# Filling TensorE's planned gaps in an attention and routing block with identity products

## The chip, the cores and the metric

One Trainium2 chip, one of its cores. The engines are PE (TensorE), DVE (VectorE), ACT (ScalarE), POOL (GpSimd) and SP (SyncE, which here only issues transfers). The metric is the device time of one launch in microseconds, as a median of runs.

## The reference

Four sequences of 1024 tokens and 256 features go through two layers. Each layer is attention and then a feed-forward part:

- layer 0: causal attention with 16 heads of 16 features, rotary embedding and a window of 64 keys; residual and layer norm; a gated feed-forward part that mixes each token with the one before it, `r * (relu(k)**2 @ W_v)`; residual and layer norm
- layer 1: linear attention over random features, `out = q_feat @ (k_feat.T @ v)`; residual and layer norm; then a block with its own layer norm, full causal attention (softmax over up to 1024 keys), another layer norm, and a mixture of 8 experts where each token goes to its two best, with 1024 places for each expert, counted in token order; a last layer norm

The order of the tokens fixes the place of each token at its expert, so the four sequences pass the router one after another.

## The kernel before, in words

The kernel has three stages: a short set-up (loads and a few transposes), the attention block that does everything up to the router for all four sequences (`attend_and_pass_on`), and the experts with the last norm. The change is in the attention block.

The block's work is cut into steps. A step is named by its kind and its place, as `("max", g, t, x)`. The 16 heads of a sequence are four groups of four; windowed and full attention of all sequences give 32 groups `g`, and each group has two halves `h` of 512 queries. The PE steps that matter here:

- `proj` (L849) projects one row tile of 128 tokens; `turn` (L868) transposes
- `max` (L876, L879, L883): scores for the row maximum. An identity times a mask first writes the mask into the bank, then the scores are added. DVE's `reduce` (L1277) reads the bank; POOL's `parts` (L1322 to L1325) splits the maximum into three bf16 parts, PE's `rows` (L889) transposes them, ACT's `lines` (L1050) copies them out, SP's `spread` sends them into `b_qk`
- `exp` (L896): the scores again, less the maximum; ACT's `power` (L1026) takes the exponential; POOL's `clear` (L1372) masks; `values` (L910) multiplies by the values; `collect`, `out` (L918) and `divide` (L1299, L1301) turn and normalise
- the layer steps: `r` (L659) and `k0` (L670) are products of the feed-forward part, `x1_turn`, `o_turn`, `oc_turn`, `h_turn` and `z_turn` (L665) are transposes of 4 times 128 x 128 in fp32, `oc_pj` (L659) is the output projection, and `logits` (L763) and `position` (L769 to L772) belong to the router. DVE's `mix_k` is L1155, the router's `place` on DVE ends at L1249

No engine decides anything at run time. A planner, `Planner.arrange`, walks a model of the block on the host: every step has a cost in us written by hand, an engine, and the steps that it comes after. It gives each engine a fixed order (`plan.program`). At each moment an idle engine takes, among the steps that are ready, the one with the longest chain behind it (`urgent`).

PSUM has eight banks of 512 fp32 columns. A PE step that fills a bank takes the one that the model frees first (`plan.bank`); `plan.after` keeps the step that had the bank before, and `left_by` names the step of DVE, ACT or POOL whose end gives the bank back. In the model a step is ready when both its inputs and a bank are there:

```python
if self.takes(x):
    b = min(bank_free, key=lambda k: bank_free[k])
    ready = max(ready, bank_free[b])
```

On PE a step of the program becomes this sequence: first `plan.wait_bank(pe, x, s)`, a wait until the bank has been read by its last reader; then the step's own waits on its inputs; then its matmuls, of which the last one increments a semaphore. PE works through its program in order.

Of the kernel before, what the change touches and what calls it, by code (L numbers as in the profile page):

```python
# [32 lines left out]
P = 128  # L33
# [19 lines left out]
CT = CAP // P  # L53
NEG = -2.0 ** 100
EPS = 1e-5
EARLY = 1
BANK = 512
DROPPED = 65536.0
# [36 lines left out]
class Planner:  # L95
# [20 lines left out]
    def add(self, x, engine, cost, *after):  # L116
        mine = self.kinds.setdefault(x[0], [])
        self.steps[x] = Step(engine, cost, [y for y in after if y is not None] + mine[-1:])
        mine.append(x)

    def arrange(self):

        steps = self.steps
        order = {x: n for k in self.kinds.values() for n, x in enumerate(k)}
        followers = {x: [] for x in steps}
        for x, st in steps.items():
            for y in st.after:
                followers[y].append(x)
        waiting = {x: len(followers[x]) for x in steps}
        urgent, ends = {}, [x for x in steps if not followers[x]]  # L130
        while ends:
            x = ends.pop()
            st = steps[x]
            urgent[x] = st.cost + max([urgent[y] + (0.0 if steps[y].engine == st.engine else self.LANDING[x[0]]
                                                    if st.engine == "SP" else self.LATE[st.engine])
                                       for y in followers[x]], default=self.AHEAD.get((x[0], x[-1]), 0.0))
            for y in st.after:
                waiting[y] -= 1
                if not waiting[y]:
                    ends.append(y)  # L140

        queues = {}
        for kind, xs in self.kinds.items():
            queues.setdefault(steps[xs[0]].engine, []).append([list(reversed(xs))])
        free_at, done, banks, bank_free = {}, {}, {}, {b: 0.0 for b in self.BANKS}
        self.program = {e: [] for e in ("PE", "DVE", "ACT", "POOL", "SP")}
        self.bank, self.after, used = {}, {}, {}
        issue_of = {self.left_by(x): x for k in self.TAKEN_BY for x in self.kinds.get(k, []) if self.takes(x)}
        now, left = 0.0, len(steps)
        while left:  # L150
            soonest, moved = None, False
            for engine, lists in queues.items():
                at = free_at.get(engine, 0.0)
                best = None
                for (q,) in lists:
                    if not q:
                        continue
                    x = q[-1]
                    if any(y not in done for y in steps[x].after):
                        continue  # L160
                    ready = max([done[y] + (0.0 if steps[y].engine == engine else self.LANDING[y[0]] if steps[y].engine == "SP"
                                            else self.LATE[steps[y].engine]) for y in steps[x].after], default=0.0)
# [3 lines that stand above are left out]
                    start = max(at, ready)  # L166
                    if start > now:
                        soonest = start if soonest is None else min(soonest, start)
                    elif best is None or urgent[x] > urgent[best[0]]:
                        best = (x, q)  # L170
                if best is not None:
                    x, q = best
                    q.pop()
                    left -= 1
                    moved = True
                    end = now + steps[x].cost
                    free_at[engine] = done[x] = end
                    self.program[engine].append(x)
                    if self.takes(x):
                        b = min(bank_free, key=lambda k: bank_free[k])  # L180
                        self.bank[x], self.after[x] = b, used.get(b)
                        used[b] = x
                        bank_free[b] = float("inf")
                    if x in issue_of:
                        bank_free[self.bank[issue_of[x]]] = end + self.LATE[engine]
            if not moved:
                assert soonest is not None
                now = soonest
        self.order = order
        self.length = max(done.values())  # L190
# [18 lines left out]
class Plan(Planner):  # L209
# [45 lines left out]
    def xa_left(self, b):  # L255


        return ("out1", 3, b - 1) if b == EARLY else self.last_projected(b, True)

# [53 lines left out]
    def describe(self):  # L313
# [14 lines left out]
        for b in range(1, B):  # L328
            add(("source", b), "SP", 6.0, ("h_turn", 1, NC - 1, b - 1))
            for y in range(2):  # L330
                for c in range(NC):
                    add(("fetch", y, c, b), "PE", 0.435, *[] if b == EARLY else [("source", b), ("out1", 3, b - 1)])
                    add(("refill", y, c, b), "ACT", 0.52, ("fetch", y, c, b))
# [57 lines left out]
        def softmax(g, h):  # L391
            mine = (g, h)
            cells = self.query_cells(g, h)
            for t, a, e in cells:
# [11 lines left out]
                if t == self.batches[b][-1][0]:  # L406
# [5 lines left out]
                *([] if self.place_of(g) else [self.known("x4_out", self.batch[g] - 2)] if windowed[g] else  # L412
                  [("o_turn", 1, EARLY), ("back", self.group_of(EARLY, True, 0), 1)] if not self.batch[g] else
                  [self.known(*x, self.batch[g] - 1) for x in (("z_out",), ("z_turn", 1, 1), ("x4", 3))]))
# [66 lines left out]
    def describe_layer(self, b):  # L481
        def add(x, engine, cost, *after, other=()):


            self.add(x + (b,), engine, cost, *[y + (b,) if y and y[0] in LAYER_KINDS else y for y in after], *other)
# [5 lines left out]
        for k in range(4):  # L491
            add(("pj", k), "PE", 1.73, ("o_take", k // 2), ("keep", near[0], k // 2))
            add(("y1", k), "DVE", 1.4, ("pj", k), other=[("source", b)] if b == EARLY else [])
        self.describe_norm(b, "n1", "y1", ("x1",))
# [58 lines left out]
        for h in range(2):  # L553
            for c in range(NC):
                before = self.last_projected(b - 1, False) if b else self.last_projected(EARLY, True)
                add(("h_turn", h, c), "PE", 0.435, ("h_act", 4 * h + 1), ("h_dve", 4 * h + 3), before)
# [32 lines left out]
def attend_and_pass_on(nc, u, s, x_dram, later, early_in, slots_gathered, slots_dram, z_dram, x4_dram):  # L589


    plan = Plan(ORDER)
# [4 lines left out]
    def o_of(g):  # L597
        return u.o if windowed[g] and plan.batch[g] != EARLY else u.y

# [43 lines left out]
    def bank_of(*x):  # L643
        return u.psum[:, plan.bank[x], :]
# [7 lines left out]
    def four(h):  # L652
        return slice(4 * h, 4 * h + 4)
# [33 lines left out]
    with nc.Block() as block:  # L687
        @block.sync
        def _(sp):
            for x in plan.program["SP"]:  # L690
                kind = x[0]
                b = x[-1]
                if kind == "source":
                    done(sp, b - 1, "h_turn", 1, NC - 1)
                    sp.dma_start(u.src[:, :, :], x_dram[b:b + 1, :, :].rearrange("o (t p) d -> p (o t) d", p=P)).then_inc(s.src_in, 16)
                elif kind == "load":
                    _, g, a, slot, y = x
                    part = [slot in slots for slots in SLOTS_OF[a]].index(True)
                    sp.wait_ge((s.high_done, s.mid_done, s.low_done)[part], 4 * (g // 2) + (4 if y is None else 2 * y + 2))
# [41 lines left out]
        def _(pe):  # L741
            for x in plan.program["PE"]:
                kind = x[0]
                if x in plan.bank:
                    plan.wait_bank(pe, x, s)
                if kind in LAYER_KINDS:
                    out = bank_of(*x)
                    x, b = x[:-1], x[-1]
# [10 lines left out]
                    elif kind == "logits":  # L759
                        done(pe, b, "z_take", 1, 1)  # L760
                        for t in range(NT):
                            for c in range(NC):
                                ins = pe.matmul(out[:, E_ * t:E_ * t + E_], u.xtr[:, c, P * t:P * t + P], u.wgate[:, c, :],  # L763
                                                start=(c == 0), stop=(c == NC - 1))
# [43 lines left out]
                    elif kind == "kv":  # L808
                        done(pe, b, "k_feat", 3)
                        done(pe, b, "v1_sum", 3)  # L810
                        for c in range(NC):
                            for t in range(NT):
                                ins = pe.matmul(out[:, P * c:P * c + P], u.kfeat[:, D * t + P * c:D * t + P * c + P],
                                                u.o[:, t, P * c:P * c + P],
                                                start=(t == 0), stop=(t == NT - 1))
# [19 lines left out]
                n = order[x]  # L835
# [34 lines left out]
                elif kind == "max":  # L870
# [4 lines left out]
                    if windowed[g]:  # L875
                        pe.matmul(out, u.id16[:, :], u.mask_q[:, :, WQ - (e - a):WQ], start=True, stop=True,  # L876
                                  skip_group_check=True)
                    elif last:
                        pe.matmul(out[:, :, P * t - a:P * t - a + P], u.id16[:, :],  # L879
                                  u.causal_q[:, :].unsqueeze(1).broadcast_to([P, len(heads), P]), start=True, stop=True,  # L880
                                  skip_group_check=True)
                    for i, h in enumerate(heads):
                        ins = pe.matmul(out[:, i, :], q[0:KS, h, P * t:P * t + P], q[0:KS, HG + h, a:e],  # L883
                                        start=not last, stop=True, skip_group_check=True)
# [6 lines left out]
                elif kind == "exp":  # L891
# [3 lines left out]
                    for i, h in enumerate(heads):  # L895
                        ins = pe.matmul(out[:, i, :], q[0:KM, HG + h, P * t:P * t + P], q[0:KM, h, a:e],  # L896
                                        start=True, stop=True, skip_group_check=True)
# [178 lines left out]
        def _(dve):  # L1076
# [11 lines left out]
            for x in plan.program["DVE"]:  # L1088
                kind = x[0]
                if kind in LAYER_KINDS:  # L1090
# [16 lines left out]
                    elif kind.endswith("_var"):  # L1107
# [6 lines left out]
                        if name == "n3":  # L1114
                            dve.tensor_scalar(w.var[:, 1, four(h)], w.mv[:, four(h), 1], 1.0 + EPS, EPS * EPS, ALU.mult, ALU.add)
                        ins = dve.tensor_scalar(w.var[:, 0, four(h)], w.mv[:, four(h), 1], EPS, None, ALU.add)
                    elif kind.endswith("_scale"):
# [554 lines left out]
def last_norm(nc, u, s, x4_dram, out_dram):  # L1672
# [4 lines left out]
    with nc.Block() as block:  # L1677
# [36 lines left out]
        def _(dve):  # L1714
            link = dve_chain(dve, s.chain)

            def statistics(h):
# [5 lines left out]
                for i in range(4 * h, 4 * h + 4):  # L1723
                    ins = dve.bn_aggr(u.last_mv[:, i, :], u.last_bn[:, i, :])  # L1724
                link(ins)
                dve.tensor_scalar(u.last_var[:, 4 * h:4 * h + 4], u.last_mv[:, 4 * h:4 * h + 4, 1], EPS, None, ALU.add  # L1726
                                  ).then_inc(s.var_ready, 1)
# [259 lines left out]
```

## Time and profile before

| | |
|---|---|
| median of 3 runs | 1914.5 us (1913.64 to 1915.02) |
| the profiled execution | 1915.56 us, span 1913.8 us |
| PE busy | 1713.6 us (90% of the span) |
| DVE, ACT, POOL busy | 1018.5, 879.8, 831.4 us |
| granted TensorE clock, mean over the span | 0.948 |

The span is the time from the first to the last instruction. The granted clock is a share of TensorE's full 2.4 GHz: 1.00 is 2.4 GHz, 0.50 is 1.2 GHz. "Idle before" in a row of the timeline is the time for which the engine had nothing to do before this instruction, and behind the arrow stands what ended it. Ends of matmuls are modelled, with the latency of each one in them, so consecutive matmuls overlap; the rate of a run of n equal matmuls is (length of the run less the length of one) over n - 1.

### The profile page before, as it was taken

The page shows a single profiled execution, that of the slowest core. Times are in us where ns is not written, and L with a number is a line of the kernel's source. Part 1 is how long each engine was busy: PE and PEld are TensorE (multiplying, and loading weights), DVE is VectorE, ACT ScalarE, POOL GpSimd, SP SyncE. Part 2 cuts the span into 40 slices and gives each one's busy share as a digit, 9 for nine tenths or more (in the row PEclk, how much of TensorE's full clock was granted, in tenths as well). Part 3 has the DMA queues.
Part 4 walks back from the last instruction along what each step waited for, and adds up shares of the span by engine and source line. Part 5 has one row for each costly group of instructions (what it writes and reads, how often), then busy time and mean ns, then how long its engine had stood idle before and what let it go on. Part 6 is the DMA issues. An engine that isn't in the chain of part 4 may idle for free. (4 is left out here: it accounts for less than half of the span.)

```text
span 1913.8 us, 32830 instructions
## 1 busy us (share of the span) xinstructions
PE 1713.6 (90%) x10804; PEld 1106.0 (58%) x10804; DVE 1018.5 (53%) x2375; ACT 879.8 (46%) x1855; POOL 831.4 (43%) x1247
## 2 busy tenths in 40 slices
PE   4798998999999999999989999998279999999970
PEld 3565765665477666556756545545246776666750
DVE  3457676868566986847698677775101110001115
ACT  2355463657755364765536566765031222222202
POOL 4574564522377552248663243324434333234220
PEclk9899999999999899999999999999589999999995
DMA  5615235032344222254502223420313332333115
GB/s 190 92 19 67 35 79 68 14 55 68 53 74 100 24 34 35 68 68 69 112 2 40 52 50 41 68 67 22 121 59 85 83 69 49 70 85 88 23 17 181
DMA packets 93059, 124.17 MB, mean 65 GB/s; under 512 B 14065, under 2 KB 63153, under 8 KB 92737
## 3 DMA queue, kind: packets, MB, share of 16 engines
q1 hardware_dynamic: 78560, 105.24, 26.8%
q0 software_dynamic: 14336, 16.83, 5.3%
q8 instruction: 94, 1.54, 0.4%
q14 instruction: 69, 0.56, 0.1%
HBM read 45.70 MB, written 25.56 MB: 37 GB/s over the span
## 5 line engine op out<-in xcount | busy, mean ns | idle before, releaser
L1026 ACT ACTIVATE b_probs<-b_psum 128x512 f32<-128x512 f32 (+3 forms) x896 | 417.9, 544 | 179.3 <-PE b_psum L896 177.7
L1277 DVE TENSOR_REDUCE b_mneg<-b_psum 128x2 f32<-128x384 f32 (+5 forms) x608 | 333.5, 593 | 94.0 <-PE b_psum L883 92.4
L1372 POOL TENSOR_SCALAR_AFFINE_SELECT b_probs<-b_probs 128x512 f32<-128x512 f32 (+1 forms) x400 | 240.0, 611 | 314.8 <-ACT b_probs L1026 304.3
L883 PE MATMUL b_psum<-b_qk 96*128 96x192 bf16 (+4 forms) x1280 | 298.9, 300 | 6.0 <-DVE b_before L1249 2.7
L896 PE MATMUL b_psum<-b_qk 99*128 99x192 bf16 (+5 forms) x1344 | 262.8, 290 | 9.7 <-DMA b_qk<-b_mrow 6.4
L1656 DVE TENSOR_TENSOR b_ye<-b_psum,b_b2b 128x512 f32<-128x512 f32 x32 | 22.1, 692 | 428.9 <-PE b_psum L1611 428.9
L1635 ACT ACTIVATE b_hid<-b_psum,b_b 128x512 f32<-128x512 f32 x128 | 88.0, 687 | 317.9 <-PE b_psum L1602 317.9
L1564 POOL DMA_INDIRECT before_last_norm<-b_ye,b_ids x64 | 99.5, 1555 | 301.0 <-DMA before_last_norm<-b_ye,b_ids 156.2
L1611 PE MATMUL b_psum<-b_w,b_hid 128*128 128x256 f32 x1024 | 222.4, 379 | 0.8 <-ACT b_hid L1635 0.8
L1602 PE MATMUL b_psum<-b_xgt,b_w 128*128 128x512 f32 x512 | 221.7, 594 | 0.0
L1611 PEld LDWEIGHTS b_psum<-b_w,b_hid 128*128 128x128 f32 x1024 | 193.9, 190 | 27.6 <-ACT b_hid L1635 1.6
L910 PE MATMUL b_psum<-b_probs,b_v 128*32 128x192 f32 (+4 forms) x2688 | 198.1, 416 | 2.3 <-POOL b_probs L1372 2.0
L883 PEld LDWEIGHTS b_psum<-b_qk 96*128 96x128 bf16 x1280 | 125.5, 101 | 100.7 <-issue 27.5
L1388 POOL TENSOR_TENSOR b_rot<-b_product 128x128 f32<-128x128 f32 x256 | 115.4, 483 | 133.4 <-DVE b_product L1260 57.1
L1277 DVE TENSOR_REDUCE b_mhalf<-b_psum 128x1 f32<-128x512 f32 x256 | 165.1, 682 | 13.1 <-PE b_psum L883 12.7
L1602 PEld LDWEIGHTS b_psum<-b_xgt,b_w 128*128 128x128 f32 x512 | 97.6, 191 | 119.4 <-issue 119.0
L896 PEld LDWEIGHTS b_psum<-b_qk 99*128 99x128 bf16 x1344 | 113.5, 98 | 88.1 <-issue 19.8
L910 PEld LDWEIGHTS b_psum<-b_probs,b_v 128*32 128x32 f32 x2688 | 69.6, 110 | 90.1 <-issue 65.0
L1260 DVE TENSOR_TENSOR b_product<-b_psum,b_cossin 128x512 f32<-128x512 f32 x128 | 87.9, 688 | 59.9 <-PE b_psum L849 54.9
L849 PE MATMUL b_psum<-b_wqkv,b_xt 128*128 128x384 f32 x320 | 116.8, 493 | 0.6 <-ACT b_xt L938 0.4
L876 PE MATMUL b_psum<-b_mask_q,b_id 128*128 128x384 bf16 (+1 forms) x256 | 84.9, 334 | 7.7 <-DMA b_qk<-b_split 5.7
L879 PE MATMUL b_psum<-b_causal_q,b_id 128*128 128x128 bf16 (+2 forms) x352 | 88.7, 252 | 3.0 <-ACT b_probs L1026 1.1
(212 smaller groups left out, 2431.6 us busy)
## 6 DMA issues: line engine op xcount, KB each, us to landing
b_qk<-b_split SPq DMA_DIRECT2D x372, 128.0 KB, 4.9
b_w<-in_W SPq DMA_DIRECT2D x16, 1024.0 KB, 7.8
b_src<-in_x SPq DMA_DIRECT2D x4, 1024.0 KB, 6.2
before_last_norm<-b_early SPq DMA_DIRECT2D x4, 1024.0 KB, 4.9
b_o<-before_last_norm SPq DMA_DIRECT2D x4, 1024.0 KB, 5.4
before_last_norm<-b_o SPq DMA_DIRECT2D x4, 1024.0 KB, 4.5
normed<-b_y SPq DMA_DIRECT2D x4, 1024.0 KB, 5.2
b_rows<-before_last_norm SPq DMA_DIRECT2D x8, 512.0 KB, 7.8
```

What stands on the lines that cost most here:

```text
L849: ins = pe.matmul(u.psum[:, plan.bank[x], 0:384].rearrange("p (a g y) -> p a g y", a=3, g=2), x_rows[:, c, P * t:P * t + P], (u.wqkv0 if n ...
L879: pe.matmul(out[:, :, P * t - a:P * t - a + P], u.id16[:, :], u.causal_q[:, :].unsqueeze(1).broadcast_to([P, len(heads), P]), start=True, ...
L883: ins = pe.matmul(out[:, i, :], q[0:KS, h, P * t:P * t + P], q[0:KS, HG + h, a:e], start=not last, stop=True, skip_group_check=True)
L896: ins = pe.matmul(out[:, i, :], q[0:KM, HG + h, P * t:P * t + P], q[0:KM, h, a:e], start=True, stop=True, skip_group_check=True)
L910: ins = pe.matmul(sums_of(g, h2)[32 * h:32 * h + 32, a - BANK * h2:e - BANK * h2], u.v[:, g % 4, t, (HD + 1) * h:(HD + 1) * h + 32], probs ...
L1026: act.activation(probs_of((g, h2, t), a, e)[:, heads[0]:heads[-1] + 1, :], bank, ACT.Exp, scale=SCALE).then_inc(s.exp_done, 1)
L1277: dve.tensor_reduce(out, in_bank(("max",) + x[1:], heads, e - a), AX.X, ALU.max, negate=True).then_inc(s.max_read, 1)
L1372: ins = pool.affine_select(out=block, in_=block, pattern=[[0, HG], [1 if ahead else -1, z - y]], compare_op=ALU.is_ge, fill=none, base=y - ...
L1388: ins = pool.tensor_tensor(out[:, :, :, HALF * y:HALF * y + HALF], straight[:, :, :, HALF * y:HALF * y + HALF], crossed[:, :, :, HALF * (1 ...
L1564: pool.indirect_dma_start(out=x4_dram, out_offset=bass.IndirectOffsetOnAxis(ap=u.ids[:, column:column + 1], axis=0), in_=u.ye[q][:, t, :], ...
L1602: ins = pe.matmul(u.psum[:, k % 4, :], u.w1[e % 2][:, c, P * n:P * n + P], u.xgt[:, c, BANK * h:BANK * h + BANK], start=(c == 0), stop=(c ...
L1611: ins = pe.matmul(u.psum[:, q, D * t:D * t + D], u.hid[:, n, P * (2 * q + t):P * (2 * q + t + 1)], u.w2[e % 2][:, n, :], start=(n == 0), s ...
```

## The change

The planner now keeps, for every step, how long its engine stood idle in the model before it (`self.idle`). When PE comes to a step that takes a bank and whose planned idle time was above 1.0 us, it issues, behind the wait for the bank and ahead of the step's own waits, a number of 128 x 128 bf16 products of the identity with itself into the first 128 columns of that bank. The step overwrites them. Their number is 0.6 of the planned idle time over 0.064 us each.

```diff
+LEAST_IDLE = 1.0
+FILLED = 0.6
+FILLER = 0.064
...
         self.bank, self.after, used = {}, {}, {}
+        self.idle = {}
...
                 at = free_at.get(engine, 0.0)
-                best = None
+                best, at = None, free_at.get(engine, 0.0)
...
                     end = now + steps[x].cost
+                    self.idle[x] = now - at
                     free_at[engine] = done[x] = end
...
                 if x in plan.bank:
                     plan.wait_bank(pe, x, s)
+                    for n in range(int(FILLED * plan.idle[x] / FILLER) if plan.idle[x] > LEAST_IDLE else 0):
+                        pe.matmul(u.psum[:, plan.bank[x], 0:P], u.id16[:, :], u.id16[:, :], start=True, stop=True,
+                                  skip_group_check=True)
```

The order of every engine and every bank stay as they were.

## Rows read from the trace of the kernel before

**Rows 1.** The page: busy time, share of the span and instructions of each engine

```profile
PE 1713.6 (90%) x10804; PEld 1106.0 (58%) x10804; DVE 1018.5 (53%) x2375; ACT 879.8 (46%) x1855; POOL 831.4 (43%) x1247
```

**Rows 2.** Stretches: length, busy time of each engine, clock, DMA share

```profile
core 0: us, PE busy (x) PEld busy (x) DVE busy (x) ACT busy (x) POOL busy (x), PEclk, DMA share, GB/s
24.00:1335.00 1311.00, 1239.03 (x9029) 783.39 (x9028) 935.92 (x2073) 747.68 (x1648) 630.49 (x1087) 0.97 0.32 56
...
51.60:54.80 3.20, 2.88 (x14) 2.00 (x15) 1.80 (x4) 0.28 (x1) 0.00 (x0) 0.50 1.00 142
58.40:61.70 3.30, 3.03 (x8) 1.86 (x9) 0.00 (x0) 0.59 (x1) 0.13 (x1) 0.50 1.07 133
89.20:99.20 10.00, 7.88 (x47) 5.88 (x48) 3.68 (x8) 3.12 (x8) 3.75 (x7) 0.50 1.07 128
154.00:157.20 3.20, 3.20 (x9) 2.67 (x10) 2.07 (x4) 1.75 (x3) 1.37 (x2) 0.50 0.12 41
174.50:177.70 3.20, 3.20 (x5) 1.23 (x4) 2.42 (x5) 0.00 (x0) 1.98 (x2) 0.50 1.06 124
300.80:307.40 6.60, 4.96 (x16) 3.46 (x15) 0.68 (x2) 0.93 (x2) 0.41 (x1) 0.50 0.62 97
...
1335.00:1403.10 68.10, 17.38 (x112) 15.73 (x113) 10.22 (x64) 7.99 (x14) 38.32 (x39) 0.50 0.41 133
```

**Rows 3.** Timeline of PE: steps whose inputs came last

```profile
44.30 0.37 PE L876 MATMUL b_psum<-b_mask_q,b_id 128*128 128x256 bf16 x1 [5.05 <-DMA b_qk<-b_split]
...
50.87 0.38 PE L889 MATMUL b_psum<-b_id,b_mparts 128*128 128x128 bf16 x4 [2.16 <-POOL b_mparts L1325]
...
58.67 0.59 PE L889 MATMUL b_psum<-b_id,b_mparts 128*128 128x128 bf16 x4 [2.50 <-POOL b_mparts L1325]
...
173.74 0.67 PE L670 MATMUL b_psum<-b_early,b_wk 128*128 128x512 f32 x1 [3.05 <-DVE b_early L1155]
```

**Rows 4.** Timeline of PE: steps whose bank came last

```profile
335.33 0.80 PE L659 MATMUL b_psum<-b_wr,b_early 128*128 128x256 f32 x1 [2.02 <-DVE b_mhalf L1277]
...
457.13 0.44 PE L665 MATMUL b_psum<-b_id,b_src 128*128 128x128 f32 x2 [0.80 <-ACT b_mrow L1050]
...
958.65 0.39 PE L883 MATMUL b_psum<-b_qk 96*128 96x512 bf16 x1 [1.97 <-DVE b_before L1249]
...
979.07 0.48 PE L659 MATMUL b_psum<-b_wr,b_early 128*128 128x256 f32 x1 [2.86 <-DVE b_mneg L1277]
```

**Rows 5.** Source view of L889: durations in ns, smallest, median, largest

```profile
L889 PE MATMUL b_psum<-b_id,b_mparts x256: 216/219/314, 50.9 to 1298.1; 128*128 128x128 bf16 x128
```

**Rows 6.** Timeline of PE: two bf16 matmuls of 128 columns, clock 0.50

```profile
44.46 0.42 PE L883 MATMUL b_psum<-b_qk 96*128 96x128 bf16 x2
```

**Rows 7.** Stretches behind the places of rows 4

```profile
338.30:456.30 118.00, 117.55 (x701) 72.76 (x700) 92.66 (x195) 71.72 (x149) 43.70 (x61) 1.00 0.22 37
457.20:512.90 55.70, 55.59 (x410) 30.52 (x410) 39.67 (x72) 39.49 (x84) 21.54 (x45) 1.00 0.21 54
638.70:655.00 16.30, 15.16 (x63) 10.14 (x63) 15.69 (x29) 3.47 (x6) 12.65 (x13) 0.79 0.04 3
```

**Rows 8.** Timeline of PE: steps with no idle time, and one behind them

```profile
517.60 0.64 PE L910 MATMUL b_psum<-b_probs,b_v 128*32 128x512 f32 x4
...
891.39 0.91 PE L896 MATMUL b_psum<-b_qk 99*128 99x64 bf16 x10 [1.08 <-DMA b_qk<-b_mrow]
```

**Rows 9.** Timeline of PE: the router's last steps; the logits of a sequence earlier

```profile
1299.15 3.64 PE L763 MATMUL b_psum<-b_wgate,b_early 128*128 128x8 f32 x32
...
1336.67 1.94 PE L665 MATMUL b_psum<-b_id,b_y 128*128 128x128 f32 x8 [6.04 <-DVE b_y L1136]
1339.65 1.94 PE L665 MATMUL b_psum<-b_id,b_y 128*128 128x128 f32 x8 [1.04 <-ACT b_y L980]
1342.55 6.97 PE L763 MATMUL b_psum<-b_wgate,b_early 128*128 128x8 f32 x32 [0.96 <-ACT b_early L938]
...
1352.83 0.17 PE L769 MATMUL b_psum<-b_chosen,b_upto 128*128 128x8 bf16 x1 [3.32 <-DVE b_chosen L1215]
```

## The prediction

> **What bounds the kernel now.** I read the page first: PE is busy for 90% of the span, DVE for 53% [rows 1]. The stretch view narrows it to the attention block, 24 to 1335 us: PE 1239 of 1311 us, DVE 936, at a mean clock of 0.97 [rows 2]. The reader is to see two losses of TensorE there: about 72 us of idle time, and 0.03 x 2 x 1311 = 79 us spent at half clock. Walking the stretch view along the block, these 79 us are 15 stretches of 3.4 to 10.2 us; six of them are shown [rows 2]. The router's last steps and the wait for the experts run at half clock altogether (1335 to 1403). Last I read the timeline of PE around each idle time, to see what ended it [rows 3, 4].
>
> A stretch at half clock of which PE is busy for b us costs at most b/2, if PE sets the time there.
>
> **What is added.** The number of fillers follows from the planner's own arithmetic, worked through with the costs in the listing: 27 steps have a planned idle time above 1.0 us and a bank. They get 493 products. No order, bank or wait changes.
>
> *Price of one.* Four bf16 matmuls of 128 columns with 128 x 128 weights take 0.38 us at full clock (at 50.87) [rows 3], one of them 0.216 [rows 5]: (0.38 - 0.216)/3 = 0.055 us each, weight load hidden. At half clock two take 0.42 us [rows 6], one 0.314 (the largest in rows 5): 0.107 us each. So 493 are 27 us of TensorE at full clock. Whether they cost anything depends on where the idle time lies relative to `wait_bank`, since they stand behind it.
>
> *(a) The step waits for its inputs (15 steps, 319 fillers).* The bank was free long before, and what ended the idle time was a transfer, POOL or DVE with an input [rows 3]. The fillers start when PE gets there: 57 before the first `max` (3.1 of 5.05 us), 30 and 32 before the first two `rows` (1.65 of 2.16, 1.76 of 2.50), 22 before `k0` (1.2 of 3.05). They fit, by 0.6 of the plan: cost 0. What hides them is the idle time itself; with it gone, they would cost 17.5 us.
>
> *(b) The step waits for its bank (8 steps, 113 fillers).* In the planner these eight start exactly when the bank comes free; in the trace the idle time before them ends with the instruction that reads the bank: `r` waits for a reduce of the maxima (L1277), `h_turn` for `lines` (L1050), `max` of group 24 for the router's `place` (L1249) [rows 4]. Here the fillers come after the idle time. The input is there, the real matmuls stand queued behind them, and behind these everything on PE. Price 113 x 0.055 = 6.2 us. Part counts in full: 22 before `r` of sequence 1, 10 and 10 before two `h_turn`, 14 before `r` of sequence 3. Behind the first two PE is busy for 117.55 of 118.0 and 55.59 of 55.7 us [rows 7], and it is as full behind the other two, so nothing takes the delay back: 56 x 0.055 = 3.1 us. The other four (11, 10, 13 and 23) lie where DVE is the fuller engine, 15.69 of 16.3 us against 15.16 for PE [rows 7]; PE waits for DVE again soon. Of their 57 x 0.055 = 3.1 us I count a third, 1.0; the bounds are 0 and 3.1.
>
> *(c) The plan has idle time, the trace has none (4 steps, 61 fillers).* PE runs later than planned, so bank and input are both there, as at the `values` at 517.60 [rows 8]. 17 fillers before a `values` at 888 are taken back by the 1.08 us that PE then waits for a transfer issued earlier (891.39) [rows 8], and 23 before a `values` at 84.6 by an idle time of POOL's making. The 11 at 517.60 count, 0.6, and half of 10 at 619, 0.3. Sum 0.9 us; bounds 0 and 3.4.
>
> Cost of (b) and (c): 3.1 + 1.0 + 0.9 = **5.0 us**, bounds 3.1 and 9.6.
>
> **What the clock gives back.** Only fillers of (a) stand in idle time, so only they can hold the clock. Of each half-clock stretch behind such a place:
>
> - 51.6 to 54.8, after 2.16 us of idle [rows 2, 3]: the 30 fillers leave 0.5 us. I take the clock as held. But DVE reads each pair of scores more slowly than a warm PE makes them, and the first transfer had only just landed, so of 2.88/2 = 1.4 us I count 0.4.
> - 58.4 to 61.7, after 2.50 us: held, 3.03/2 = 1.5, PE is then busy without a break; 1.3.
> - 89.2 to 99.2: DMA share 1.07, PE waits for transfers; 0.2 of 3.9.
> - 154 to 157.2, only 11 fillers ahead: one chance in three of 1.6; 0.55.
> - 174.5 to 177.7, after 3.05 us with 22 fillers: 0.4 of 1.6; 0.6.
> - 300.8 to 307.4: 9 fillers, at the edge of it, of 2.5; 0.4.
>
> The first fall, at 41.3 us, gives nothing: behind it PE waits for transfers. The eight other stretches follow places of (b), or places without fillers. Sum: 3.45 us, bounds 0 and (2.88 + 3.03 + 7.88 + 3.20 + 3.20 + 4.96)/2 = 12.6.
>
> *The router's end.* Everything from `z_turn` to `place` of the last sequence is one chain, and it runs at half clock: its logits take 6.97 us where those of the sequence before took 3.64 [rows 9]. The 30 fillers in the 6.05 us before it end 4 us too early to hold the clock. But 15 and 12 fillers between the two `z_turn` and the logits make PE busy without a break for 6 us. TensorE came back to full clock after such runs elsewhere (58.4 to 61.7, PE busy 3.03 of 3.3). I expect full clock for somewhat over half of the logits: 2.0 of 3.3 us. Against it, at half clock 15 x 0.107 = 1.6 us fill a gap of 1.04, less the 0.2 by which transposes overlap: 0.35 late, 0.1 more before the logits, and 35 x 0.107 = 3.75 in the 3.32 before `position`, 0.2. Net gain **1.4 us**, bounds -0.7 (no return of the clock) and 3.3.
>
> **The sum.** 5.0 - 3.45 - 1.4 = +0.15 us. Against the profiled execution of 1915.56 us that is 1915.7; this execution lies 1.06 above the median of the runs, so 1914.65, **1914.7 us** as a median.
>
> **A rule against the change.** After idle times of 2.16 and 2.50 us TensorE fell to half clock [rows 2, 3]. The Trainium skill, page "TensorE: Matmul & The Clock Gate", section "Why this matters for your kernels", asks only that there be no idle gaps over about 3 us between bursts. By this trace shorter ones matter too; by the page, the fillers in 23 of the 27 places would protect nothing. As a mechanism of this kernel: only the four idle times above 3 us (44.30, 173.74, 1336.67, 1352.83) [rows 3, 9] bring a gain, 0.6 + 1.4, and the rest only cost: 5.0 - 2.0 = +3.0, 1917.5 us.
>
> **The rivals.**
>
> - *Faster: the clock is worth its full price.* Every one of the six stretches is held and PE sets the time in all of them: 5.0 - 12.6 - 1.4 = -9.0, 1905.5 us. For it: PE is 78 to 100% busy in five of the six. Against it: the DMA share of 1.07 in two of the largest, the few fillers before 154 and 300.8. It decides from gains of 8.8 us up.
> - *Slower: the fillers do not hold the clock*, so the change doesn't do what it is built for. Gains 0, the router's end 0.7 late: 5.0 + 0.7 = +5.7, 1920.2 us. For it: they cover only 0.6 of the planned gap, and the largest delays of (b) sit where PE is full. Against it: bf16 products with the mask ran from 44.30 us at half clock [rows 3, 6], and by 50.87 four products took the 0.38 us of full clock: such products bring the clock back. If DVE hides nothing either, 9.6 + 0.7, 1924.8 us. It decides when less than 1.2 of the 4.85 us comes.
> - *The rule above*: 1917.5 us.
> - *The router's end only loses*: 5.0 - 3.45 + 0.7, 1916.8 us.
>
> **How the numbers follow.** A measurement of this kernel can tell from no change about 0.2%, 3.8 us. The forecast has 0.50, the faster rival 0.15, no hold of the clock 0.20 (0.04 of it at the far value), the rule 0.08, the router's end 0.07. Faster: 0.15 and 0.02 from the forecast's edge, 0.17. Slower: 0.20 and 0.02, 0.22. Within: 0.61. The range leaves out most of the faster rival and the far value: 1908.5 to 1921.0. The forecast's own is 1911 to 1918.
>
> **What would show it.** The trace of after should have: fillers at 0.055 us each, 22 of them directly behind the idle time before `r` of sequence 1, which stays 2 us, and `r` 1.2 us later than the work before it; no idle time in front of fillers in the first `rows`; full clock after about 51 and 58 us, half clock still after about 335, 618, 936 and 960; the last logits in about 5 us. The prediction is wrong if the stretches of (b) disappear too, if DVE's places take back no delay, or if PE-full stretches turn out to have slack.

## The result, and the profile after

The changed kernel took 1904.39 us (median of 6 runs, 1900.55 to 1911.71) beside 1914.76 us for the kernel before (6 runs, 1913.3 to 1916.6): ratio 0.9947, 95% interval 0.9927 to 0.9966. That is 10.4 us faster, and below 1908.5, the low end of the range. It was measured twice more, in the experiments below, and came out less: 0.9977 (0.9963 to 0.9990) and 0.9965 (0.9952 to 0.9978). All 30 runs of it have a mean of 1907.1 us (standard error 0.7), all 98 runs of the kernel before 1913.3 (0.3): **6.2 us, 0.32%, faster**. The first figure was a good draw of the one against a poor draw of the other. That the changed kernel is faster, by more than the 0.2% that the prediction called the least that can be told, holds in the mean of all runs.

The profiled execution of after is the slowest of its six, 1911.71 us, span 1910.0. It is read here for places, not for the total. The page, as [rows 1]:

```profile
PE 1731.8 (91%) x11297; PEld 1130.5 (59%) x11297; DVE 1017.4 (53%) x2375; ACT 879.0 (46%) x1855; POOL 828.5 (43%) x1247
```

PE has 11297 - 10804 = 493 more matmuls, as counted from the planner. The stretch view of after, as [rows 2]; the columns are those shown there:

```profile
24.00:1334.00 1310.00, 1254.72 (x9459) 804.43 (x9459) 935.07 (x2073) 746.99 (x1649) 627.89 (x1087) 0.98 0.32 56
54.10:57.30 3.20, 3.20 (x20) 2.46 (x19) 3.04 (x7) 0.00 (x0) 0.00 (x0) 0.50 1.08 123
91.60:98.20 6.60, 6.17 (x34) 4.93 (x35) 3.09 (x6) 2.73 (x7) 3.76 (x6) 0.50 1.07 129
146.20:149.40 3.20, 2.77 (x24) 2.16 (x24) 1.63 (x4) 2.16 (x4) 1.74 (x3) 0.50 0.00 0
171.20:177.20 6.00, 5.97 (x20) 3.77 (x21) 4.67 (x13) 1.59 (x3) 3.89 (x4) 1.00 1.07 126
296.40:303.00 6.60, 5.87 (x25) 4.68 (x24) 0.68 (x2) 1.13 (x2) 0.62 (x1) 0.50 0.59 94
1334.00:1402.00 68.00, 23.12 (x180) 20.59 (x181) 9.94 (x64) 9.72 (x15) 39.96 (x41) 0.55 0.42 137
```

The mean clock of the block rose to 0.98. The half-clock stretches at 58, 154 and 174 us are gone, the one at 89 is shorter, that at 51 stands at 54, that at 300 is still there, and one stands at 146 where there was none.

The timeline of PE; the fillers are L752. First places where the input came last, as [rows 3]:

```profile
44.96 0.28 PE L884 MATMUL b_psum<-b_mask_q,b_id 128*128 128x256 bf16 x1 [2.49 <-DMA b_qk<-b_split]
...
47.41 1.84 PE L752 MATMUL b_psum<-b_id 128*128 128x128 bf16 x30
50.28 0.40 PE L897 MATMUL b_psum<-b_id,b_mparts 128*128 128x128 bf16 x4 [1.03 <-POOL b_mparts L1333]
...
56.57 2.34 PE L752 MATMUL b_psum<-b_id 128*128 128x128 bf16 x32
58.79 0.40 PE L897 MATMUL b_psum<-b_id,b_mparts 128*128 128x128 bf16 x4
...
168.12 1.39 PE L752 MATMUL b_psum<-b_id 128*128 128x128 bf16 x22
171.23 0.70 PE L675 MATMUL b_psum<-b_early,b_wk 128*128 128x512 f32 x1 [1.72 <-DVE b_early L1163]
```

Thirty take 1.84 us: (1.84 - 0.22)/29 = 0.056 us each. They lie at the front of the idle time, and the rest of it (1.03, 1.72) stays. Before the second `rows` (58.79) none stays: there the first part of the 32 ran at half clock, and they took 2.34 us. In `e9_again`, at full clock, they took 1.95 and left 1.14. Then places where the bank came last, as [rows 4]:

```profile
331.10 2.53 PE L752 MATMUL b_psum<-b_id 128*128 128x128 bf16 x22 [2.02 <-DVE b_mhalf L1285]
333.42 0.65 PE L664 MATMUL b_psum<-b_wr,b_early 128*128 128x256 f32 x1
...
453.94 0.73 PE L752 MATMUL b_psum<-b_id 128*128 128x128 bf16 x10 [0.80 <-ACT b_mrow L1058]
454.50 0.50 PE L670 MATMUL b_psum<-b_id,b_src 128*128 128x128 f32 x3
...
957.78 2.02 PE L752 MATMUL b_psum<-b_id 128*128 128x128 bf16 x23 [1.98 <-DVE b_before L1257]
959.59 0.64 PE L891 MATMUL b_psum<-b_qk 96*128 96x512 bf16 x1
```

Here the same idle time as before, 2.02, 0.80 and 1.98 us, stands ahead of the first filler, and the real matmul follows the last filler directly. The router's end, as [rows 9]:

```profile
1335.40 1.94 PE L670 MATMUL b_psum<-b_id,b_y 128*128 128x128 f32 x8 [4.39 <-DVE b_y L1144]
1337.13 1.81 PE L752 MATMUL b_psum<-b_id 128*128 128x128 bf16 x15
1338.73 1.91 PE L670 MATMUL b_psum<-b_id,b_y 128*128 128x128 f32 x8
1340.44 1.00 PE L752 MATMUL b_psum<-b_id 128*128 128x128 bf16 x12
1341.52 4.58 PE L771 MATMUL b_psum<-b_wgate,b_early 128*128 128x8 f32 x32
1345.95 3.89 PE L752 MATMUL b_psum<-b_id 128*128 128x128 bf16 x35
```

The logits take 4.58 us where they took 6.97. The 35 fillers after them ran at half clock, 3.89 us, and leave no idle time before `position`.

### The profile page after: what moved, and what is told of

The parts are those of the page before. It is cut to its first block and busy times, and to the rows that moved or that the text cites. A ratio compares the mean times of both kernels' runs of the same rounds, so it can differ in the third digit from the quotient of the medians.

```text
span 1910.0 us, 33797 instructions
## 1 busy us (share of the span) xinstructions
PE 1731.8 (91%) x11297; PEld 1130.5 (59%) x11297; DVE 1017.4 (53%) x2375; ACT 879.0 (46%) x1855; POOL 828.5 (43%) x1247
```

## The experiments

Twelve kernels ran, ten of them with other fillers and two unchanged copies of the changed kernel. Each has a ratio against runs of the kernel before on the same chip. "Half-clock time" is 2 x (1 - granted clock) x span, as a mean over all timed runs of a kernel; it is 193.5 us for the kernel before (92 runs) and 153.8 us for the changed one (30 runs). It includes what lies behind the block: in the profile of before 68 us from 1335 on, the router's last steps and the wait for the experts, and 53 us from 1861 to the end, where PE is idle.

**Input or bank.** The planner also keeps how long the bank was free before the step started; `e1_inputs` takes one sign of it, `e2_bank` the other.

```diff
+                        self.bank_early[x] = now - bank_free[b]
...
-... if plan.idle[x] > LEAST_IDLE else 0):
+... if plan.idle[x] > LEAST_IDLE and plan.bank_early[x] > 0.01 else 0):     # e2_bank: <= 0.01
```

> Only the 19 steps whose bank is free before their inputs in the plan get their fillers (380); the 8 whose bank comes last get none. Theory A, the 113 fillers behind a bank wait are a delay of 3 to 5 us and the rest gives all of the gain: ratio to before about 0.992 (-13 to -15 us). Theory B, the fillers at those 8 steps also keep the clock, or their delay is taken back by waits for DVE: about 0.9945 or worse (-10 us or less).

> Only the 8 steps whose bank comes last get their 113 fillers. Theory A: +3 to +5 us (ratio 1.0015 to 1.0025), and the clock falls where it fell before. Theory B: between -3 and +1 us, with fewer falls of the clock.

Measured: `e1_inputs` 1901.53 us, 0.9936 (0.9914 to 0.9957); half-clock time 156 us. `e2_bank` 1917.02 us, 1.0025 (1.0012 to 1.0038), 4.8 us slower; half-clock time 192 us, as before. `e1_inputs` alone does not decide: it lies between the numbers of the two theories, and its interval holds both. `e2_bank` decides for theory A, as it lies in A's +3 to +5 us and outside B's: behind a bank wait the fillers are delay, and over whole runs they hold no clock. A row of `e2_bank`, timeline of PE:

```profile
334.75 2.53 PE L753 MATMUL b_psum<-b_id 128*128 128x128 bf16 x22 [2.03 <-DVE b_mhalf L1286]
337.07 1.14 PE L665 MATMUL b_psum<-b_wr,b_early 128*128 128x256 f32 x2
```

**By region.** A counter `pe_step` over PE's program limits the places: `pe_step < 100` for `e3_start`, `pe_step > 2500` for `e4_end`, and between them with an early bank for `e5_middle`.

```diff
-            for x in plan.program["PE"]:
+            for pe_step, x in enumerate(plan.program["PE"]):
...
+... and pe_step < 100 else 0):
```

> Only the five places before 90 us get fillers (160). The prediction's sum gave 1.9 us for them. If a kept clock is worth its full price at the start, the stretches at 51.6, 58.4 and 89.2 give up to 6.9 us: ratio 0.9965. If transfers and DVE set the time there, -1 to -2 us, 0.9993.

> Only the router's last four steps get fillers (92). The prediction's sum: -1.4 us, logits in about 5 us. If the clock is back for all of the logits, -2.5 to -3 us; if it never comes back, +0.7 us.

> Only the ten places between 100 and 1330 us whose bank is early get fillers (128). The prediction's sum: 1.55 us of clock against 0.9 of delay, -0.7 us. What the runs with all early banks, the start alone and the end alone leave for them (12.2 less 2.7 less 1.7): about -8 us, ratio 0.996.

Measured: start 0.9986 (0.9971 to 1.0001), -2.7 us, half-clock time 176 us; end 0.9991 (0.9974 to 1.0007), -1.7 us, 186 us; middle 0.9970 (0.9956 to 0.9984), -5.7 us, 182 us. The first two are not clear of nothing by themselves. The middle is, and lies far above the 0.7 us of the prediction, if below the 8 us that the other runs left for it.

**Only real gaps, and more of them.** `e6_real_gaps` drops the four places of (c) as well. `e7_more` has `FILLED = 0.9`; `e8_more_places` adds `LEAST_IDLE = 0.4` to that, and asks for a bank that is early by more than 0.2 us (not shown): 30 places, 620 fillers.

```diff
+... and plan.bank_early[x] > 0.01 and pe_step not in (84, 854, 1068, 1589) else 0):
...
-FILLED = 0.6
+FILLED = 0.9     # e7_more and e8_more_places
```

> As e1_inputs, without the four places of (c) where the trace has no idle time (15 places, 319 fillers). If those 61 fillers are a delay of 0.9 to 3.4 us: -13 to -15 us against before, ratio 0.9925. If they also keep the clock: -12 or less.

> The 15 places with 0.9 of the planned idle time in place of 0.6 (about 480 fillers). If the clock is what pays: fewer half-clock us than e6_real_gaps, and 1 to 3 us faster than it. If the fillers now outrun the gaps: as fast or slower than it.

> As e7_more, and also places with a planned idle time of 0.4 to 1.0 us whose bank is early (some 15 more). If the clock pays: the fewest half-clock us of all, -15 to -18 us, ratio 0.991. If short gaps have no bearing on the clock: as e7_more.

Measured: `e6_real_gaps` 1903.81 us, 0.9955 (0.9939 to 0.9972), half-clock time 156; `e7_more` 1907.93 us, 0.9975 (0.9964 to 0.9985), 157; `e8_more_places` 1906.08 us, 0.9953 (0.9934 to 0.9971), 146. None of the three came as far as its expectation with the clock paying (-13 to -15, 1 to 3 us below `e6_real_gaps`, -15 to -18). In `e7_more`, half as many fillers again held no more clock and lost time; its profile shows them outrunning gaps (48 before the second `rows`, with no idle time left). The additional places of `e8_more_places` did lower the half-clock time, by 10 us, and its mean time is 3.6 us below that of `e7_more` (standard error 1.6) and 0.6 above that of `e6_real_gaps` (1.9). The delay is that of the 0.9; the additional places with 0.6 were not tried.

**The changed kernel again, and the logits.** `e9_again` is an unchanged copy. `e10_logits` is `e6_real_gaps` with two fillers between the row tiles of each logits step.

```diff
                         for t in range(NT):
+                            for n in range(2 if t else 0):
+                                pe.matmul(out[:, BANK - P:BANK], u.id16[:, :], u.id16[:, :], start=True, stop=True,
+                                          skip_group_check=True)
```

> The changed kernel once more, beside runs of the kernel before on the same chip. The steps whose length the profiles give (start -3.3, 126 to 230 -1.7, 430 to 500 -1.5, router's end -2.3, bank waits +3) sum to -5.8 us; the first measurement gave -10.4. If the sum is right and the first measurement fell on slow runs of the kernel before: -5 to -8 us, ratio 0.996 to 0.997. If a gain is missing from the sum: 0.995 or less.

> As e6_real_gaps, and two identity products ahead of each of the last seven row tiles of every logits step (14 a step, 56 in all), where PE is busy with products of 8 columns and the clock falls behind them at 613, 933 and 1297 us. If it is the clock that pays, and the columns that TensorE streams hold it: fewer half-clock us by 10 to 15, and 2 to 5 us faster than e6_real_gaps. If busy time alone counts: 14 x 0.055 x 4 = 3.1 us slower, half-clock time as before.

Measured: `e9_again` 1907.61 us, 0.9977 (0.9963 to 0.9990). `e10_logits` 1905.25 us, 0.9961 (0.9945 to 0.9978), half-clock time 160: no better than `e6_real_gaps` in either. In its profile the clock still fell during the logits, at 614 and 935 us. The fall at 1270 stands in another place, where PE waited 2.46 us for a transfer; and behind the logits of 1299 the kernel before had no fall in its profile either. A miss: so few products do not hold the clock there, and whether more would pay was not tried.

**The best version.** All early banks but the `values` at 84.6 us, and the changed kernel beside it.

> The 18 places whose bank is early, without the values step at 84.6 us, whose 23 fillers cost 1.28 us in the profiles. Sum of the segments: -8.8 us against before, ratio 0.9954, and 3 us faster than the changed kernel beside it. If the fillers behind bank waits cost nothing in whole runs: as the changed kernel.

> The changed kernel, unchanged, beside e11_best on the same chip. Sum of the segments: -5.8 us, ratio 0.997. The first measurement would be 0.9947.

Measured: `e11_best` 1902.22 us, 0.9931 (0.9916 to 0.9945); `e12_third` 1906.08 us, 0.9965 (0.9952 to 0.9978). The intervals do not meet: without the fillers behind bank waits the kernel is faster. (`e11_best` also lacks the 23 at 84.6; `e1_inputs` has them and is as fast.) Together the 18 runs of `e1_inputs`, `e6_real_gaps` and `e11_best` have a mean of 1902.75 us (standard error 0.8), 4.35 us below the changed kernel and 10.6 below the kernel before.

**What a fall costs.** The fourteen profiles (before, after, twelve runs) give one more experiment for nothing: the order of PE's steps is the same in all, so the time from the start of one step to the start of another can be set side by side. Where the clock does not fall it repeats closely: 344.0 to 453.6 us is 109.4 to 109.6 in all fourteen. Lengths in us, from the starts in the timelines; "without" is for four kernels that have no fillers there (always before and `e2_bank`, and two of `e3_start`, `e4_end` and `e5_middle`), "changed" for its three profiles (after, `e9_again`, `e12_third`):

| stretch of the kernel before | without | changed | counted in the prediction |
|---|---|---|---|
| 44.30 to 51.92 (first `max` until the second transfer) | 7.63, 8.15, 7.66, 7.69 | 7.71, 7.74, 7.73 | 0 |
| 51.92 to 58.67 (second `max` to its `rows`) | 6.75, 7.38, 7.38, 7.38 | 6.12, 5.74, 5.74 | 0.4 |
| 58.67 to 72.6 (`rows`, then 14 steps of the projection) | 13.92, 14.10, 15.17, 14.93 | 12.42, 12.43, 12.49 | 1.3 |
| 72.6 to 107.81 | 35.22, 34.19, 34.33, 33.66 (the last has the 9 ahead of 107.81) | 35.28, 33.31, 34.11 | 0.2 for 89 |
| 107.81 to 152.16 | 44.35, 44.36, 44.93, 44.36 | 45.49, 44.28, 44.27 | in the 0.55 for 154 |
| 152.16 to 173.74 | 21.57, 19.90, 20.53, 19.91 | 19.25, 19.90, 19.90 | the rest of it |
| 173.74 to 178.94 (two `k0`) | 5.21, 5.21, 5.15, 3.51 | 3.54, 3.54, 3.54 | 0.6 |
| 303.78 to 330.9 | 27.15, 27.51, 28.18, 28.11 | 26.99, 25.31, 25.31 | 0.4 |
| 1336.67 to 1352.83 (`z_turn` to `position`) | 16.16, 16.16, 16.16, 16.16 | 14.24, 14.49, 12.14 | 1.4 |

The two `k0` are the cleanest: 5.15 to 5.21 us at half clock, 3.51 to 3.54 at full, whatever else the kernel has (in one kernel without fillers the clock happened to be full there). And one that has no fillers in any kernel, from 1099.5 to 1117.6 us: 18.01 to 18.02 us in the four profiles where the clock fell in it, 16.55 to 16.57 in the ten others. One fall of 3.4 us costs 1.45 to 1.67 us here, nearly half of it, where PE is full.

The same profiles tell whether the fillers or luck kept the clock. Each stretch has four kernels without the fillers ahead of it and ten with them. From 58.67 to 72.6 the clock fell or was down for a time in all four, and in none of the ten. At the two `k0` it was three of four and none of ten, from 51.92 to 58.67 four of four and six of ten, from 303.78 to 330.9 four of four and four of ten. From 1336.67 to 1352.83 it was down throughout in the four, and for part of the time in the ten.

The same view prices the bank waits. From 330.9 to 344.0 us, across `r` of sequence 1, it is 13.06, 13.32, 13.33, 13.32 us without, and 14.12, 14.49, 14.50, in `e2_bank` 14.40, with the 22 fillers: 1.1 us. The clock was down for 3.4 to 3.5 us in all of these, and the fillers themselves took 2.53 us in two of them: part of the work that ran at half clock without them ran at full clock behind them. Three kernels without these fillers were no faster there (`e1_inputs`, `e10_logits`, `e11_best`: 14.65 to 14.68), as the clock was down for 6.8 us; why is not known. The stretch from 453.6 to 561.3 us is 107.5 to 107.7 without and 108.12 in `e2_bank`, with the 10 before `h_turn`: 0.5 us.

## Why the prediction was wrong

Point by point, by its own steps.

- *Price of one filler*: 0.055 us counted, 0.056 measured; at half clock (2.53 - 0.31)/21 = 0.106, counted 0.107. Right.
- *(a) They cost nothing in the idle time before an input*: right at 0.6 of the plan where they run at full clock (152.16 to 173.74, with the 22 before `k0`, is 19.90 us with and without them); wrong at 0.9.
- *(b) The bank waits*: right in place, mechanism and size. Counted 4.1 us; `e2_bank` measured 4.8, and the runs without them are 4.35 us faster than those with them. Single places: 1.1 for 1.2, 0.5 for 0.55.
- *(c) Places without idle time*: 0.9 us counted. The 23 before the `values` at 84.6 delay it by 1.28 us, and the idle time behind takes it back, as the prediction had it: from 58.67 to 107.81 us `e9_again`, with them, took 45.74 us and `e6_real_gaps`, without, 46.02. (The clock was down for 3.4 us of it in both.) The expectation of `e11_best`, that they cost 1.28 us of the whole, was wrong. `e6_real_gaps` is not faster than `e1_inputs`: the other three cost too little to be seen.
- ***What the clock gives back* is the step that failed.** The prediction: "Sum: 3.45 us, bounds 0 and (2.88 + 3.03 + 7.88 + 3.20 + 3.20 + 4.96)/2 = 12.6", and 1.4 for the router's end, 4.85 together. Measured: the changed kernel's 6.2 us and the 4.35 that its bank waits cost are 10.6 us of gain. The table has 9.9 of them, each as the mean of without less the mean of changed. By the prediction's terms: 1.4 for 0.4 counted (51.6), 2.1 for 1.3 (58.4), 0.1 for 0.2 (89.2), 0.6 for 0.55 (154), 1.2 for 0.6 (174.5), 1.9 for 0.4 (300.8), and 2.5 for 1.4 (the router's end). The rest, 0.7, is less than the standard error of the 10.6 (0.9).

The mechanism stood, so the sum was mis-sized, in four ways. The first: a discount for another engine. For 51.6 us it said "DVE reads each pair of scores more slowly than a warm PE makes them ... I count 0.4". In `e9_again` the clock is full there (timeline of PE):

```profile
52.83 0.32 PE L884 MATMUL b_psum<-b_mask_q,b_id 128*128 128x384 bf16 x1 [2.03 <-DMA b_qk<-b_split]
...
55.32 0.33 PE L891 MATMUL b_psum<-b_qk 96*128 96x192 bf16 x2
55.48 1.95 PE L752 MATMUL b_psum<-b_id 128*128 128x128 bf16 x32
58.58 0.40 PE L897 MATMUL b_psum<-b_id,b_mparts 128*128 128x128 bf16 x4 [1.14 <-POOL b_mparts L1333]
```

From 52.83 to the fillers PE did not wait once, so DVE did not hold it back. Against the 6.75 us of the kernel before, the 5.74 here are 1.0 less; the mean of 1.4 is higher because in the three others without fillers the clock was down for longer. The second: chances. At 174.5 and 300.8 the clock was given "0.4" and "at the edge of it". In the changed kernel's three profiles it was held at the `k0` three times of three and behind 303.78 two times of three. The third: the router's end, where over half of the logits at full clock was counted as 2.0 us of them, and they came out 2.1 to 3.2 shorter. The fourth: the list of falls came from one execution of a kernel whose falls move; two of its own runs differ by up to 13.8 us (1907.63 to 1921.45). Behind 58.67 that execution took 13.92 us, 1.5 above the changed kernel, as counted; the other three without fillers took 14.10 to 15.17.

Two terms came out near their numbers by luck. For 154 the fall was absent in two of the four without fillers and moved to 146 in one of the three with them. For 89.2 the reason given was that transfers set the time. But in the changed kernel the clock was still down for 3.4 to 6.8 us there, and in `e8_more_places`, the only profile in which it was not down at all, the stretch took 31.91 us, 2.4 less than without fillers. How much of that is the clock is not shown, as that kernel has other fillers there.

The rivals: "faster, the clock is worth its full price" is nearest to what happened, at 10.6 us of its 14.0; it took the clock as held in all places, and at 89 us and in part of the profiles at 51.6 and 300.8 it was not. "The fillers do not hold the clock" fell with `e1_inputs` (193.5 to 156 us of half-clock time). The rule of the Trainium skill, page "TensorE: Matmul & The Clock Gate", section "Why this matters for your kernels", asks for no idle gaps over about 3 us. That shorter ones do no harm does not hold in these runs: the gap of 2.50 us before 58.67 was followed by half clock in the kernel before, and with fillers in it in none of ten profiles, worth 2.1 us. "The router's end only loses" fell: 4.58, 4.84 and 3.74 us of logits for 6.97.

That a kept clock is the cause of the gain is shown where the same steps are shorter by half a fall and the clock differs. That the fillers kept it, rather than luck in when it falls, is shown by the counts: none of ten profiles against four of four behind 58.67, and 154 us of half-clock time in 30 runs against 194 in 92. Why the clock falls at a gap in one execution and not in the next stays open.

## What to carry to other kernels

Work put into an engine's idle time costs nothing only if it may start when the idle time starts: ask of every gap which wait ends it, the input or the buffer, for filling behind a wait for the buffer is pure delay. When TensorE is full on both sides of a gap, price a fall of its clock near half of the busy time that follows (here 1.45 to 1.67 us for 3.4), and take off something for another engine only if it holds TensorE back at full clock. And a forecast about the clock needs several executions of the kernel before; one profile is one draw.

## What the runs showed that was not expected

- A fall of the clock is not tied to the program alone. The same kernel was profiled at 1911.71 and at 1901.92 us; from 24 to 1330 us the second had 37 us at half clock, the first 55, and half of the difference, 9 us, is most of the 9.8.
- Within the runs of one kernel the time rises by 0.29 us (before) and 0.39 us (changed) for each us of half-clock time. Between the two kernels it is (6.2 + 4.35)/(193.5 - 153.8) = 0.27.
- The three runs of the kernel before that were shown at first lay within 1.4 us; 98 spread over 13.8, with a standard deviation of 2.5.
- The clock can fall although PE is busy without a break: in the kernel before PE was busy for 3.20 of the 3.20 us ahead of the fall at 935.6 us, and for 3.19 of 3.20 ahead of that at 618. In both the work was in good part the logits, fp32 products of 8 columns. That they are the reason is not shown: behind the same products at 1299 us the clock did not fall in that profile.
